# A four-layer convolution kernel on Trainium2: the turn between images of the third stage reordered, and the convolution's residual adds moved from GpSimd to VectorE

## The reference

```python
x = x + L0(_gn(x))   # 3x3 convolution of sign(x) with ternary weights
x = x + L1(_gn(x))   # rfft2, mixing of channels per frequency, irfft2
x = x + L2(_gn(x))   # 7x7 convolution, padding 3, bias
x = x + L3(_gn(x))   # attention in windows of 8x8, 8 heads of 8, then a projection
```

## Time and profile before

| | |
|---|---|
| median of 3 runs | 11607.0 us (11600.54 to 11622.02) |
| profiled execution, its own time | 11606.86 us |
| its span, first to last instruction | 11605.2 us |
| granted TensorE clock, mean | 0.946 |
| TensorE matmul busy | 88% |
| VectorE busy | 71% |
| ScalarE busy | 51% |
| GpSimd busy | 34% |

### The profile page before, as it was taken

How to read it: one execution, slowest core, us unless ns; L and a number is a source line. 1 busy time by engine, 2 the same in 40 slices (tenths; PEclk the granted TensorE clock), 3 DMA queues, 4 the chain that set the end, 5 groups by cost and what they waited for, 6 DMA issues and landing times.

```text
span 11605.2 us, 293145 instructions
## 1 busy us (share of the span) xinstructions
PE 10197.8 (88%) x121127; PEld 9029.9 (78%) x121127; DVE 8258.5 (71%) x13913; ACT 5931.6 (51%) x7185; POOL 3908.2 (34%) x3388
## 2 busy tenths in 40 slices
PE   7898967776999999999999999999999999999996
PEld 5777767776888888888888888888888888888884
DVE  7777733333677777777777777777777777777775
ACT  4666631112455555555555555555555555555553
POOL 0000000001444444444444444444444444444442
PEclk9999987776999999999999999999999999999996
DMA  8999989992011111111111111111111111111100
GB/s 205 241 240 241 241 197 236 236 231 63 21 35 33 34 34 34 32 42 32 32 35 35 32 35 33 34 35 34 35 32 36 38 32 33 34 35 32 35 22 17
DMA packets 666939, 903.58 MB, mean 78 GB/s; under 512 B 479698, under 2 KB 595266, under 8 KB 642434
## 3 DMA queue, kind: packets, MB, share of 16 engines
q1 hardware_dynamic: 635675, 664.91, 25.7%
q0 software_dynamic: 29952, 220.22, 5.2%
HBM read 547.41 MB, written 322.96 MB: 75 GB/s over the span
## 4 chain that ended last, share of the span: by engine, by line
PE 43%; DVE 13%; issue 8%; ACT 8%; POOL 3%; DVEq 0%; ACTq 0%; POOLq 0%; DMA 0%; SPq 0%
PE c_ps L1156 25%; PE c_ps L1218 5%; DVE c_xp L1680 3%; POOL c_cube L2003 2%; PE c_ps L1292 2%; PE c_ps L1202 2%; PE c_ps L1186 2%; PE c_ps L1231 2%; ACT c_sq L1470 2%; ACT c_xp L1416 2%; PE c_ps L1239 1%; DVE c_s L1781 1%; ACT c_sq L1478 1%; PE c_ps L1279 1%; DVE c_tn L1673 1%
## 5 line engine op out<-in xcount | busy, mean ns | idle before, releaser
L1156 PE MATMUL c_ps<-c_xp,c_wst 128*128 128x224 f16 x45696 | 4894.6, 264 | 318.1 <-DVE c_xp L1680 218.0
L1156 PEld LDWEIGHTS c_ps<-c_xp,c_wst 128*128 128x128 f16 x45696 | 4351.5, 98 | 772.4 <-issue 315.8
L2003 POOL TENSOR_TENSOR c_cube<-c_sq,c_qk 128x896 f32<-128x896 f32 x448 | 939.2, 2117 | 2219.3 <-ACT c_sq L1470 2219.3
L638 PE MATMUL b_ps<-b_wt,b_xt 64*64 64x64 f32 x12768 | 729.4, 285 | 328.9 <-DVE b_xt L613 185.5
L1680 DVE TENSOR_TENSOR c_xp<-c_tn,c_xp 128x1080 f16<-128x1080 f32 (+1 forms) x560 | 784.3, 1412 | 290.9 <-ACT c_xp L1416 289.5
L638 PEld LDWEIGHTS b_ps<-b_wt,b_xt 64*64 64x64 f32 x12768 | 711.7, 169 | 346.5 <-issue 346.1
L1979 POOL TENSOR_TENSOR c_xr<-c_sm,c_xr 128x448 f32<-128x448 f32 x448 | 710.5, 1586 | 689.6 <-DVE c_xr L1698 689.6
L1416 ACT ACTIVATE c_xp<-c_tn 128x1080 f16<-128x1080 f32 (+1 forms) x560 | 581.1, 1057 | 706.8 <-DVE c_tn L1673 702.7
L1712 DVE TENSOR_TENSOR c_qk<-c_ps,c_bqk 128x512 f32<-128x512 f32 (+1 forms) x896 | 556.7, 621 | 528.2 <-PE c_ps L1218 491.6
L1403 ACT ACTIVATE c_tn<-c_xr,c_nrm 64x448 f32<-64x448 f32 (+2 forms) x800 | 910.0, 1141 | 27.0 <-DVE c_xp L1680 12.7
L1965 POOL TENSOR_TENSOR c_tn<-c_tn 128x224 f32<-128x224 f32 (+1 forms) x480 | 352.8, 735 | 1643.3 <-ACT c_tn L1403 1301.2
(11 more groups left out here) (166 smaller groups left out, 17365.6 us busy)
## 6 DMA issues: line engine op xcount, KB each, us to landing
b_wt<-in_L_conv_weight SPq DMA_DIRECT2D x28, 4096.0 KB, 42.5
a_xc<-in_x SPq DMA_DIRECT2D x64, 1568.0 KB, 21.8
x<-a_x1s POOLq DMA_DIRECT2D x64, 1568.0 KB, 11.7
a_xh<-x SPq DMA_DIRECT2D x64, 1568.0 KB
out<-c_xr SPq DMA_DIRECT2D x448, 224.0 KB, 3.1
c_xr<-x SPq DMA_DIRECT2D x192, 448.0 KB, 3.4
b_xs<-xf SPq DMA_DIRECT2D x28, 2048.0 KB, 23.8
yf<-b_ys POOLq DMA_DIRECT2D x112, 512.0 KB, 9.8
```

Source lines behind the costliest of these rows:

```text
L638: ins = pe.matmul(ps[C * half:C * half + 2 * B, 4 * half + g % 4, at:at + C], xt[rows, u, f, 1 - r:3 - r].rearrange("p r b -> p (r b)"), w ...
L1156: ins = pe.matmul(sums(c, p), wst[:, ws, pr, FIRST_TAP[p] + k].rearrange("p q o -> p (q o)"), xp[:, xs, PLANE[kind] + f, row:row + CROWS, ...
L2003: pool.tensor_tensor(cube[:, :, k].rearrange("p q r c -> p r q c"), sq[:, :, :, k], qk[:, :, :, k], ALU.mult).then_inc(done, 1)
```

## The change

- The adds of the convolution's products become VectorE's: `add_products` takes the place of `add_conv`. The first pair of a chunk stands behind takes 4 and 5, ahead of `x3_stats` and the second sum of squares; the second pair behind takes 6 to 8, ahead of the masking of the key-value product.
- On VectorE the second split of a row stands behind that masking.
- In the turn VectorE's and ScalarE's lists have the first planes earlier, between the parts of attention. For odd next images the third block's repeated ring rows are written alone, without waiting for the last products, with semaphores of their own (`edge_high`, `edge_low`), and its other four rows after that (`high_rows`, `low_rows`, the latter behind `x3_norm`). ScalarE's zero rows come ahead of the deviation. GpSimd makes the fourth plane ahead of the attention's output.
- TensorE makes the statistics after 80 matmuls of an image, not 70.
- In row 5 ScalarE and VectorE turn some groups of the inverse transform earlier.

```diff
-FIRST_STATS_AT = 70
+FIRST_STATS_AT = 80
...
                     elif c == 0 and p == 0 and i == 3 * taps:
-                        pe.wait_ge(s.lo_done, n * NCH + 3)
+                        if odd:
+                            pe.wait_ge(s.edge_low, n + 1)
+                        else:
+                            pe.wait_ge(s.lo_done, n * NCH + 3)
...
                 halves = HALF_ROWS[0:1] if k < EARLY else HALF_ROWS
-                zero_rows(k, HALF_ROWS if k == 0 else halves)
+                if k:
+                    zero_rows(k, halves)
...
-                elif k == (2 if odd else 4) and above_zero(n):
+                elif k == (3 if odd else 4) and above_zero(n):
                     act.wait_ge(s.prod_done, n * A7 * NP)
+                if k == 2 and odd:
+                    (at, rows), (edge, few) = ring(k, odd)
+                    act.activation(xp[:, 0, :, edge:edge + few].rearrange("p k j w -> p k (j w)"),
+                                   tn[:, k % 2, 0:9, 0:few].rearrange("p k j w -> p k (j w)"), ACT.Copy).then_inc(s.edge_high, 2)
+                    return
                 for at, rows in ring(k, odd):
                     ins = act.activation(xp[:, 0, :, at:at + rows].rearrange("p k j w -> p k (j w)"),
                                          tn[:, k % 2, 0:9, 0:rows].rearrange("p k j w -> p k (j w)"), ACT.Copy)
                 ins.then_inc(s.hi_done, 1)
+
+            def high_rows(n):
+                act.wait_ge(s.prod_done, n * A7 * NP)
+                act.activation(xp[:, 0, :, 0:ROWS].rearrange("p k j w -> p k (j w)"),
+                               tn[:, 0, 0:9].rearrange("p k j w -> p k (j w)"), ACT.Copy).then_inc(s.hi_done, 1)
...
                 act.activation(sq[:], cube[:].rearrange("p q k r c -> p r q k c"), ACT.Square).then_inc(s.u6_done, 1)
+                middle()
                 if a < A7 - 1:
                     window_rows(l + 1, a + 1, odd)
-                middle()
                 act.wait_ge(s.ratio_done, l + 1)
                 act.activation(fac[:], fac[:], ACT.Sqrt).then_inc(s.f_done, 1)
+                between()
                 act.wait_ge(s.qt_done, l + 1)
...
+                act.wait_ge(s.c2_done, CHUNKS * (n + 2))
+                zero_rows(0, HALF_ROWS)
                 deviation(2 * n + 1)
                 padded_chunk(n + 1, 1 - odd, 0)
                 padded_chunk(n + 1, 1 - odd, 1)
                 take_b(n, A7 - 1, True)
                 take_b(n, A7 - 1, False)
+                high_part(n + 1, 1 - odd, 0)
                 if attention:
                     turned(n * A7 - 1)
-                high_part(n + 1, 1 - odd, 0)
                 high_part(n + 1, 1 - odd, 1)
                 padded_chunk(n + 1, 1 - odd, 2)
                 if attention:
                     give(n * A7 - 1)
                 padded_chunk(n + 1, 1 - odd, 3)
                 high_part(n + 1, 1 - odd, 2)
+                if not odd:
+                    high_rows(n + 1)
                 deviation(2 * n + 2)
                 act.wait_ge(s.rstd_done, 2 * n + 3)
                 window_rows(n * A7, 0, odd)
...
+                if k == 2 and odd:
+                    (at, rows), (edge, few) = ring(k, odd)
+                    dve.wait_ge(s.edge_high, n + 1)
+                    dve.tensor_tensor(xp[:, 1, :, edge:edge + few].rearrange("p k j w -> p k (j w)"),
+                                      tn[:, k % 2, 0:9, 0:few].rearrange("p k j w -> p k (j w)"),
+                                      xp[:, 0, :, edge:edge + few].rearrange("p k j w -> p k (j w)"), ALU.subtract
+                                      ).then_inc(s.edge_low, 2)
+                    return
...
+            def low_rows(n):
+                dve.wait_ge(s.hi_done, n * NCH + 3)
+                dve.tensor_tensor(xp[:, 1, :, 0:ROWS].rearrange("p k j w -> p k (j w)"),
+                                  tn[:, 0, 0:9].rearrange("p k j w -> p k (j w)"),
+                                  xp[:, 0, :, 0:ROWS].rearrange("p k j w -> p k (j w)"), ALU.subtract).then_inc(s.lo_done, 1)
...
+            def add_products(n, odd, c, half):
+                chunk = n * A7 + c
+                here = phases(xr, odd, c)[:, 2 * half:2 * half + 2]
+                apart = lambda t: t.rearrange("p (j i) -> p j i", j=CROWS)
+                dve.wait_ge(s.t_taken, NT * chunk + HALVES * (half + 1))
+                dve.tensor_tensor(here, apart(sm[:, half]).unsqueeze(1).to_broadcast([P, 2, CROWS, QW]), here, ALU.add
+                                  ).then_inc(s.added, 1)
+                dve.wait_ge(s.added, 2 * chunk + (half + 1))
+                ins = dve.tensor_tensor(here, bs[:, 0:2].rearrange("p f (j i) -> p f j i", j=CROWS), here, ALU.add)
+                if half:
+                    ins.then_inc(s.x3_done, 1)
+
...
@@ -1786,12 +1834,12 @@
                 dve.tensor_tensor(fac[:, :, 0], fac[:, :, 0], s6[:, :, 0], ALU.mult)
                 dve.tensor_tensor(fac[:, :, 1], fac[:, :, 1], s2[:, :, 1], ALU.mult).then_inc(s.ratio_done, 1)
                 pad("low", 0)
+                late(2)
                 dve.wait_ge(s.f_done, l + 1)
                 dve.tensor_tensor(keys, keys, fac[:, :, 1].rearrange("p (r q) -> p r q", r=2).unsqueeze(3).to_broadcast(
                     [P, 2, Q7, C]), ALU.mult).then_inc(s.scaled, 1)
                 late(0)
                 pad("differ", 1)
-                pad("low", 1)
                 late(1)
                 if above_zero(l):
                     dve.wait_ge(s.xo_done, l)
@@ -1799,6 +1847,7 @@
                     dve.wait_ge(s.kv_done, 2 * l + (w + 1))
                     dve.tensor_tensor(kvm[:, w], ps[:, 4 + w, 0:HEADS * Q7].rearrange("p (q x) -> p q x", q=Q7),
                                       head[:].unsqueeze(1).to_broadcast([P, Q7, HEADS]), ALU.mult).then_inc(s.kvm_done, 1)
+                pad("low", 1)
...
                 padded_low(n, odd, k)
@@ -1830,22 +1879,27 @@
                 if attention:
                     divide(row)
                     multiply(row)
+                differ(n + 1, 0)
+                if attention:
                     add_depthwise(row)
+                differ(n + 1, 1)
                 take_t(n, odd, A7 - 1, 3)
-                differ(n + 1, 0)
-                differ(n + 1, 1)
+                low_part(n + 1, after, 0)
+                padded_low(n + 1, after, 2)
                 take_t(n, odd, A7 - 1, 4)
                 take_t(n, odd, A7 - 1, 5)
-                low_part(n + 1, after, 0)
-                padded_low(n + 1, after, 2)
                 low_part(n + 1, after, 1)
+                padded_low(n + 1, after, 3)
                 for p in range(6, NP):
                     take_t(n, odd, A7 - 1, p)
                 differ(n + 1, 2)
-                padded_low(n + 1, after, 3)
+                add_products(n, odd, A7 - 1, 0)
                 low_part(n + 1, after, 2)
+                add_products(n, odd, A7 - 1, 1)
                 x3_stats(n, odd, A7 - 1)
                 x3_norm(n, 2 * n + 2)
+                if after:
+                    low_rows(n + 1)
                 differ(n + 1, 3)
...
+                    add_products(n, odd, a, 0)
 
                 def late(a, at):
+                    if at == 2:
+                        if more and a == A7 - 2:
+                            turn_c1(n + 1, ROW5_TURNED[0:1])
+                        return
                     if more and a == A7 - 1:
                         add_x2(n + 1, 1 - odd, *ROW6_X2[2 + at])
                     elif more and a == A7 - 2:
+                        if at == 0:
+                            add_products(n, odd, a, 1)
                         if at == 1:
-                            turn_c1(n + 1, ROW5_TURNED)
+                            turn_c1(n + 1, ROW5_TURNED[1:])
                     elif at == 0:
                         take_t(n, odd, a, 6)
                         take_t(n, odd, a, 7)
                         take_t(n, odd, a, 8)
+                        add_products(n, odd, a, 1)
...
                 differ(n + 1, 2)
-                add_conv(n, odd, A7 - 1, 0)
-                add_conv(n, odd, A7 - 1, 1)
+                differ(n + 1, 3)
                 if attention:
                     add_out(n * A7 - 1, A7 - 1, 1 - odd)
-                differ(n + 1, 3)
                 differ(n + 1, 4)
...
-                        add_conv(n, odd, a, 0)
```

More of the change, by code:

```diff
@@ L972, in large_conv_and_attention @@
             proj_done o2_done xo_done dw_taken bn3_done x2_copied x2_put
[L973 removed]
+            c1_turned x1_end x2_moved tn_cleared edge_high edge_low""".split()
         s = type("Semaphores", (), {n: sem(n) for n in names})
@@ L1460, in give, with attend @@
                 ins.then_inc(s.o2_done, 1)
-            def attend(l, a, odd, begin, middle, high, end):
+            def attend(l, a, odd, begin, middle, between, high, end):
                 begin()
@@ L1559, in end @@
                             if more and a == A7 - 2:
```

(11 more changed lines are left out.)

19 lines of the change are left out of this document (3 added, 16 removed).

## The result

| | before | after |
|---|---|---|
| median | 11612.6 us (6 runs, 11600.54 to 11625.41) | 11654.77 us (6 runs, 11648.11 to 11668.52) |
| profiled execution's span | 11605.2 us | 11648.0 us |

The ratio is 1.0037, with a 95% interval from 1.0024 to 1.005: the change makes the kernel slower by 0.37%, some 42 us, or 1.4 us if it is divided by the 30 images that have a next one. The forecast was 147 us: 4.7 for each of these images and 6 for the last one.

A forecast was written before the change was run, and what follows sets the result against it. TensorE was taken to bound rows 1 to 4, VectorE the turn and row 0. A loss of 4.7 us per image made 141 over 30 images, plus 6 for the last: 11750 us, 1.2% slower, range 11430 to 11840.

The forecast's parts named there:

- the term for rows 1 to 4: Attention rows 1 to 4: VectorE becomes the bound, 32.4 us against 30.9, each row 1.5 longer, 6.0 for four.
- The price of an add: A strided add of 448 elements on VectorE takes 1.03 us, so 4.1 us for a chunk's four.
- The collisions: In rows 1 to 4 the first add waits 1.2 us for GpSimd's cubes, the second 2.05 for its output add.
- the sum of 4.7: Loss per image in us: +6.0 + 0.5 - 0.8 - 1.0 = 4.7, making 141 for 30 images.
- The list of 32.4: Rows 1 to 4: VectorE's work and waits of 31.4 us plus 1.00 waiting for ScalarE's squares.
- In these rows I cost it at nothing: Rows 1 to 4: moving the split behind the key-value product doesn't shorten VectorE's list, so it is worth nothing.
- Turn -1.0: Turn between images: 2.7 us won to an odd next image, 0.7 lost to an even one, mean 1.0 won.
- row 0 -0.8: Row 0: the moved split removes a 3.0 us wait for one parity, the adds give most back; 0.8 us won.
- row 5 +0.5: Row 5: earlier spectrum turning wins what the adds cost in front of it; +0.5 us, between -1.5 and +2.
- Rival B: Gains and losses cancel: turn -3, rows lose 1.0 each, 0.7 us per image, 11630 give or take 60; chance 0.15.

The follow-up runs named there:

- turn_only: The changed kernel with all adds given back to GpSimd at their earlier places, the other edits kept: 11348.88 us, ratio 0.9779 to the kernel before.
- pair_late: The changed kernel with each row's first pair of adds moved behind takes 6 to 8, where GpSimd is idle: 11545.91 us, ratio 0.9946 to the kernel before.
- out_later: The changed kernel with GpSimd's output add held until VectorE's first pair of adds is done, in each row but the last: 11474.58 us, ratio 0.9888.

## Why the prediction was right and wrong

- **Direction and bound, right; size, wrong.** Slower, and by the mechanism it named: in rows 1 to 4 VectorE became the bound, through the price of the adds and through GpSimd's hold on the operands. turn_only shows the two together, and pair_late and out_later the second part: without collisions the adds' own 4 us fit into the row. But the loss was 42 us and not 147. The step that failed is the size of the term for rows 1 to 4.
- **The price of an add, right.** 1.03 us was taken; 0.96 to 1.00 undisturbed was measured. Half of GpSimd's 1352 ns, which the Trainium skill (GPSIMD Engine Reference, Key points) would give, is 0.68; VectorE's shortest was 957 ns, so for this strided pattern the factor is 1.4, and the measurement decides.
- **The collisions, right.** 1.2 and 2.05 us were named, 1.19 (2.17 - 0.98) and 1.80 (2.78 - 0.98) came. out_later shows that it is the overtaking output add.
- **Rows 1 to 4, the term that was mis-sized.** "+6.0", 1.5 in each of four rows, was +3.6, in the two images of the table as over all 29. That is 2.4 of the 3.9 us per image by which the sum of 4.7 was off; row 5 has 1.0 of the rest and the turn 0.75. The list of 32.4 was 0.5 too long (some 0.2 for four adds at 0.98, 0.25 for the second collision, 0.1 for the wait): the plain row is 31.9. And the 1.5 was laid on every row, also on those that had a wait for the product already. Rows 1 to 4 of the odd image were 32.3, 30.9, 30.9 and 31.9 and became 31.9, 33.5, 31.9 and 31.7: in rows 1 and 4, where the split of two pieces stood ahead of the product, the new bound takes the old wait's place and costs nothing, while the split itself, now behind the product, lengthens row 2 and goes into row 5, which has room.
- **"In these rows I cost it at nothing", wrong.** The split's place was worth 612 us, 20 per image, with the adds on VectorE, and 122 to 138 without. The reason given was that the row is as long as VectorE's list wherever the split stands. The list of 32.4 charged neither the 1.25 of waiting for ScalarE's high part nor the gap behind the product, and so assumed what only the moved split brings about. This error did not enter the sum, and that was luck: a list without these waits was the right one for this order, and would have missed 20 us per image for the other.
- **Turn -1.0, row 0 -0.8, row 5 +0.5:** measured over all 29 images -1.75, -0.70 and -0.47. In the turn VectorE reaches the statistics 25.4 us (6276.98 to 6302.4) after the numerator, where 26.7 was forecast, and 25.7 to the even image; but to that even image TensorE then takes 6.4 to the projection, not 4.8, at the lower clock; in all but three of the 30 turns it is 4.9 to 5.1. Row 5 gains because the other edits, of which the earlier spectrum turning is the one in this row, win 3.5 there and more than pay for the adds.
- **What was not seen:** that the other edits alone are a gain of 257 us. The forecast netted them against the adds stretch by stretch. Rival B came nearest, with 0.7 per image and 11630 give or take 60, and in part for another reason: its rows at +1.0 each came about (0.9), its turn at -3 did not.

## What to carry to other kernels

Where two engines hand work to each other once a row, ask of each operation whether it stands ahead of the hand-over or behind it. Behind, it fills the time in which its engine would wait for the answer; ahead, it is in the loop with all that it waits for, and its place can be worth several times its length once the engine is full: 4.1 us of a row here, for a split of 1.28. Move work onto another engine only after such places are used, and keep pairs of dependent operations away from the moment at which the neighbour has an access queued. When a change has several parts, test each with and without the costly one: here two cheap reorderings won 2.2%, and the move of the adds gave all of it back and more.
